# Three output blocks of the inner feed-forward layers in turns, each turn a scheduled step, and a new table of places

## The reference, cut to what matters

```python
def reference(x, ...):                         # x: (4, 1024, 256), fp32
    x = x + 0.5 * ffn(layernorm(x))
    x = x + attn(layernorm(x))
    x = x + 0.5 * ffn(layernorm(x))            # the same weights again
    return x

def ffn(x):                                    # weights are -1, 0 or 1, with one scale for each output
    h = silu((x @ w1.T) * s1) * ((x @ w2.T) * s2)      # 256 -> 1024
    h = gelu((h @ h1.T) * t1)                          # 1024 -> 1024, the first inner layer
    h = gelu((h @ h2.T) * t2)                          # 1024 -> 1024, the second inner layer
    return (h @ w3.T) * s3                             # 1024 -> 256

def attn(x):                                   # 16 heads of 16; each row looks back at 24 fixed offsets
    q, k, v = split(x @ Wqkv + bqkv)
    p = softmax(q . k[row - offset] / 4 + pos_bias)    # offsets 0 .. 768, causal
    return (sum(p * v[row - offset]) * sigmoid(x @ Wgate + bgate)) @ Wout + bout
```

## Time and profile before

| what | value |
|---|---|
| time, median of 3 runs | 1644.64 us (1642.39 to 1644.68) |
| the profiled execution's own time | 1643.29 us |
| its span | 1641.1 us |
| PE busy | 1514.2 us, 92% of the span |
| DVE, ACT, POOL busy | 66%, 41%, 34% |
| weights through the ring | 256 fills of 512 KB |

### The profile page before, as it was taken

How to read it: one execution, slowest core, us unless ns; L and a number is a source line. 1 busy time by engine, 2 the same in 40 slices (tenths; PEclk the granted TensorE clock), 3 DMA queues, 4 the chain that set the end, 5 groups by cost and what they waited for, 6 DMA issues and landing times.

```text
span 1641.1 us, 19144 instructions
## 1 busy us (share of the span) xinstructions
PE 1514.2 (92%) x6914; PEld 1215.0 (74%) x6914; DVE 1088.8 (66%) x1477; ACT 678.3 (41%) x1061; POOL 553.5 (34%) x402
## 2 busy tenths in 40 slices
PE   0399999999999999999999999889999999998998
PEld 0288787778777778787777777768788877776887
DVE  4423678886587867777977775869675978783322
ACT  4434344434343435444424343434343534342442
POOL 0111142516044425243426152351705254425020
PEclk9999999999999999999999999999999999999999
DMA  9633657676657575666855667547574766754332
GB/s 376 259 118 119 210 169 255 226 249 213 208 188 268 171 258 192 228 239 205 308 181 203 209 203 241 189 164 266 180 253 153 283 238 210 271 191 145 131 99 76
DMA packets 191008, 342.38 MB, mean 209 GB/s; under 512 B 15552, under 2 KB 138560, under 8 KB 190784
## 3 DMA queue, kind: packets, MB, share of 16 engines
q1 hardware_dynamic: 190912, 341.13, 60.9%
HBM read 310.66 MB, written 30.41 MB: 208 GB/s over the span
## 4 chain that ended last, share of the span: by engine, by line
PE 74%; DVE 9%; POOL 7%; DMA 4%; issue 3%; ACT 3%; SPq 0%; DVEq 0%; POOLq 0%; ACTq 0%
PE f_bank L1020 25%; PE f_bank L1021 24%; PE a_bank L1096 6%; PE f_bank L981 5%; PE f_bank L982 5%; PE f_bank L1049 3%; POOL acc L630 3%; PE f_bank L1050 3%; DMA slot<-in_ffn_w 2%; PE a_bank L1114 2%; DVE S L886 2%; DVE slot L880 2%; POOL acc L627 1%; POOL h_lo L644 1%; DVE slot L924 1%
## 5 line engine op out<-in xcount | busy, mean ns | idle before, releaser
L1020 PE MATMUL f_bank<-h_hi,wring 128*128 128x512 f32 x2048 | 824.6, 403 | 21.7 <-POOL h_lo L644 12.0
L1021 PE MATMUL f_bank<-h_lo,wring 128*128 128x512 f32 x2048 | 814.0, 397 | 0.0
L1020 PEld LDWEIGHTS f_bank<-h_hi,wring 128*128 128x128 f32 x2048 | 388.0, 189 | 120.2 <-POOL h_lo L644 16.1
L1021 PEld LDWEIGHTS f_bank<-h_lo,wring 128*128 128x128 f32 x2048 | 388.0, 189 | 93.7 <-issue 1.7
L714 ACT ACTIVATE h_hi<-f_bank,colv 128x512 fp32r<-128x512 f32 x256 | 176.0, 688 | 537.0 <-PE f_bank L1021 536.6
L840 DVE TENSOR_TENSOR h_lo<-f_bank,h_hi 128x512 fp32r<-128x512 f32 x256 | 175.4, 687 | 255.3 <-ACT f_bank L715 253.9
L644 POOL TENSOR_TENSOR h_lo<-f_gated,h_hi 128x512 fp32r<-128x512 f32 x128 | 166.3, 1311 | 501.0 <-ACT h_hi L708 500.8
L981 PE MATMUL f_bank<-fT_hi,w_in 128*128 128x512 f32 x512 | 212.1, 414 | 27.1 <-issue 10.9
L982 PE MATMUL f_bank<-fT_lo,w_in 128*128 128x512 f32 x512 | 206.1, 402 | 0.0
L924 DVE TENSOR_TENSOR slot<-slot,a_bank 128x1280 f32<-128x1280 f32 (+4 forms) x124 | 169.8, 1376 | 20.2 <-DMA slot<-keys_and_values 20.0
L880 DVE TENSOR_TENSOR slot<-slot,a_bank 128x1280 f32<-128x1280 f32 (+4 forms) x124 | 170.6, 1375 | 16.3 <-DMA slot<-keys_and_values 16.1
(11 more groups left out here) (92 smaller groups left out, 1191.4 us busy)
## 6 DMA issues: line engine op xcount, KB each, us to landing
wring<-weights_hi SPq DMA_DIRECT2D x256, 512.0 KB, 4.7
slot<-keys_and_values SPq DMA_DIRECT2D x128, 384.0 KB, 4.7
slot<-keys_and_values SPq DMA_DIRECT2D x64, 640.0 KB, 4.2
slot<-keys_and_values SPq DMA_DIRECT2D x312, 128.0 KB, 4.5
slot<-keys_and_values SPq DMA_DIRECT2D x64, 256.0 KB, 5.5
slot<-in_ffn_w SPq DMA_DIRECT2D x22, 512.0 KB, 6.8
weights_hi<-h_hi SPq DMA_DIRECT2D x16, 512.0 KB, 6.1
keys_and_values<-kv_out SPq DMA_DIRECT2D x32, 256.0 KB, 2.7
```

Source lines behind the costliest of these rows:

```text
L1020: pe.matmul(bank[:, :], hi, h_hi[src][:, k, :], start=(k == 0), stop=False)
L1021: last = pe.matmul(bank[:, :], hi, h_lo[src][:, k, :], start=False, stop=(not general and k == KH - 1))
```

## The change

`f_hidden` of the first three blocks of each inner layer is cut in two steps. A new PE step `f_begin` (r, layer, m) for m = 0, 1, 2 does k = 0..5 (12 matmuls); then the steps `f_hidden` m = 0, 1, 2 do k = 6, 7 (4 matmuls each). Before, one step held 28 matmuls (m = 0 and 1), then 4, then 16; now there are steps of 12, 12, 12, 4, 4, 4. Since attention steps are put in at boundaries of PE steps, they may now stand between these. The waits are those of before, and stand with the first part of a block; the number of matmuls is the same, and so is every transfer. The ring's fill times follow `f_begin`. `f_gelu`, `f_lo` of m = 0 and 1 and `f_stats` follow the later planned end of m = 0 and 1. `TIMES`, `FOLLOW` and `STARTS` have new numbers, of which these lines are a part.

```diff
-TIMES = [4.0, 9.6, 11.1, 13.4, 16.0, 24.8, 22, 3.8, 5.6, 53.0, 58.4, 3.1, 86.9, 3.5]
+TIMES = [3.8, 9.6, 11.1, 16.4, 18.6, 27.1, 23.3, 3.8, 6.4, 53.0, 60.2, 3.3, 89.2, 3.5]
-FOLLOW = dict(silu=-1.5, gate=0.1, cut=1.3, low=2.0, gelu=-0.4,
-              lo=1.0, residual=-1.5, residual2=0.4, fill=20.7, stats=0.1, turn=4)
+FOLLOW = dict(silu=-1.5, gate=-0.4, cut=1.3, low=1.3, gelu=-0.4,
+              lo=1.3, residual=-1.5, residual2=0.2, fill=20.7, stats=0.0, turn=4)
...
+    ABREAST = 3
...
                 for layer in range(2):
+                    for m in range(ABREAST):
+                        pe(2.8, "f_begin", r, layer, m)
                     for m in range(KH):
-                        done = pe([6.5, 0.95, 3.7][min(m, 2)], "f_hidden", r, layer, m)
+                        done = pe(0.95 if m < ABREAST else 3.7, "f_hidden", r, layer, m)
+                        if m < ABREAST:
+                            begin["f_hidden", r.j, layer, m] = begin["f_begin", r.j, layer, m]
...
-            def run_hidden(r, layer, m, ring, general):
+            def run_hidden(r, layer, m, early, ring, general):
...
-                if general or m > 1:
-                    part(m, 0, KH)
-                elif m == 0:
-                    part(0, 0, EARLY)
-                    part(1, 0, EARLY)
-                    part(0, EARLY, KH)
+                if general:
+                    if not early:
+                        part(m, 0, KH)
+                elif early:
+                    part(m, 0, EARLY)
                 else:
-                    part(1, EARLY, KH)
+                    part(m, EARLY if m < ABREAST else 0, KH)
```

More of the change, by code:

```diff
@@ L30 @@
          "z", "out"]
-TIMES = [4.0, 9.6, 11.1, 13.4, 16.0, 24.8, 22, 3.8, 5.6, 53.0, 58.4, 3.1, 86.9, 3.5]
-FOLLOW = dict(silu=-1.5, gate=0.1, cut=1.3, low=2.0, gelu=-0.4,
-              lo=1.0, residual=-1.5, residual2=0.4, fill=20.7, stats=0.1, turn=4)
-STARTS = [86, 164, 237, 328, 401, 468, 552, 632,
-          703, 783, 862, 941, 1021, 1102, 1173, 1251]
+TIMES = [3.8, 9.6, 11.1, 16.4, 18.6, 27.1, 23.3, 3.8, 6.4, 53.0, 60.2, 3.3, 89.2, 3.5]
+FOLLOW = dict(silu=-1.5, gate=-0.4, cut=1.3, low=1.3, gelu=-0.4,
+              lo=1.3, residual=-1.5, residual2=0.2, fill=20.7, stats=0.0, turn=4)
+STARTS = [86, 164, 237, 328, 401, 468, 554, 632,
+          703, 781, 862, 938, 1027, 1102, 1173, 1251]
 class Counts:
@@ L1122, in run @@
                     "f_in": lambda r, m: run_in(r, m, ring, general),
-                    "f_hidden": lambda r, layer, m: run_hidden(r, layer, m, ring, general),
+                    "f_begin": lambda r, layer, m: run_hidden(r, layer, m, True, ring, general),
+                    "f_hidden": lambda r, layer, m: run_hidden(r, layer, m, False, ring, general),
                     "f_out": lambda r: run_out(r, ring, general),
```

## The result

The changed kernel takes 1653.77 us in the median of 5 runs (1652.39 to 1657.51), the kernel before 1644.68 us (1642.39 to 1646.13): a ratio of 1.0056, 95% interval 1.0042 to 1.007. It is slower by 9.1 us (0.6%), where a gain of 3.7 was forecast.

What follows compares the result with a forecast made beforehand. PE, busy 92%, was taken as the bound, with 81 us between its matmuls to act on. Gains of 28.4 us less costs of 24.7 net 3.7, giving 1640.9 us from the median; forecast range 1634 to 1648, overall 1625 to 1654.

Steps and rivals of the forecast that it cites:

- pass 14, `f_low` 7: POOL does `f_low` 7 straight behind `f_low` 6, so PE's wait and half-rate loss there go: gain 9.0 us.
- second residual: End of pass 3: the second `f_residual` now precedes a score, shortening waits into pass 4: gain 3 us, bounds 1 to 4.5.
- pass 9 to 10, and 321, 819: Layer 1's block 4 waits less behind a10's scores, gain 4 us; similar waits at 321 and 819, gain 3 together.
- pairs at once: PE waits out evictions when `a_turn` meets kv0 or `a_z_turn` its `a_out`; 9 pairs become 16: cost 5.2 us.
- `a_tanh`: Passes 8 and 13: ACT does `a_tanh` ahead of `f_scale`, so `f_turn` waits: cost 7 us, 3.5 each.
- `a_exp`: Passes 5 and 10: `a_exp` and table loads come between `f_gelu` 1 and 2, delaying `f_scale` and `f_turn`: cost 4.5 us.
- a11's `a_turn`: Pass 10: reached 24 matmuls into the layer instead of 48, so PE waits for `a_hat`: cost 4 us, bounds 0 to 7.
- ring: Slot 0 is freed later while block 4 is due as before, giving waits of 1.1 and 0.4: cost 1 us.
- Rival C: Ring fills queue behind SP's other waits, 26 layers x 0.3 us at block 4: no difference, 1649 us; chance 0.08.
- Rival B: Reordered ACT and POOL steps decide, new gaps bring half-rate windows: slower, about 1651 us; chance 0.22.
- Rival A: New stalls are swallowed, since PE's waits let DVE and POOL catch up: about 1630 us; chance 0.25.
- Rival D: The third block does nothing without a late `f_low`, leaving only the places; already in the sum, no chance of its own.

Runs made afterwards that it cites:

- e4: The changed kernel with `f_scale` ahead of `a_tanh` in passes 8 and 13, on ACT's order alone: 1649.78 us, 1.0034.
- e5: The changed kernel with `f_stats`, `f_rstd` and `f_scale` planned 2.8 us earlier (stats=-2.8): 1650.7 us, 1.0031.
- e15: The changed kernel with three blocks in turn in layer 0 and only two in layer 1: 1645.44 us, 1.0001.
- e3: The changed kernel with two blocks in turn instead of three, as steps of their own, new places kept: 1645.01 us, 0.9997.
- e6: The changed kernel with `f_stats`, `f_rstd` and `f_scale` planned 4.1 us earlier (stats=-4.1): 1665.29 us, 1.0113.
- e8: The changed kernel with stats=-4.1 and the ring's transfers for blocks 4 and 12 planned 3.2 us earlier in SP's order: 1665.53 us, 1.0126.
- e12: The changed kernel with the third block doing only k = 0 to 3 in its turn, so block 0 ends 0.93 us earlier: 1640.4 us, 0.9968.
- e13: The changed kernel with a third block of 4 k in its turn and `f_turn` one block later (turn=5): 1634.84 us, 0.9936.
- e18: The changed kernel with a third block of 2 k in its turn and `f_turn` one block later (turn=5): 1633.14 us, 0.9928.
- e9: The changed kernel with `f_turn` one block later (turn=5) and the bank waits that belong to it: 1641.76 us, 0.9981.

## Why the prediction was wrong

Each term, with what the changed kernel's trace gives. A gap is counted here, as in the expectations, from start to start of PE's instructions less the undisturbed pace, which is 0.1 to 0.2 us more than the idle time in brackets. Gaps and the clock behind them are counted together; a stretch of 3.41 us at half rate is 1.7 us.

| step of the prediction | forecast | found |
|---|---|---|
| pass 14, `f_low` 7 | gain 9.0 | 9.0: no wait near 1480, no half-rate stretch |
| pass 9, cover | gain 1.4 | 1.4: one wait for POOL is left, in pass 5 |
| second residual | gain 3 | 4.6: in pass 4 4.55 us became 1.60, and its stretch is gone; pass 3 waits 0.8 longer |
| pass 11 | gain 4.5 | 3.4: 1.7, 2.5 and a stretch became 1.6 and 1.0 |
| pass 9 to 10, and 321, 819 | gain 7 | 13: 4.5, 2.0 and 3.7 became 0.7, 0 and 2.2, and three stretches (1.7, 1.7 and 2.2 us) went |
| `a_z_turn` and `a_turn` | gain 3.5 | 0.4 |
| pairs at once | cost 5.2 | 4.3 (waits for aT and zT) |
| `a_tanh` | cost 7 | 7.2 in the trace; undone, 3.6 (e4) |
| `a_exp` | cost 4.5 | 8.0: 2.80 twice with two stretches, less 1.0 of before |
| a11's `a_turn` | cost 4 | 7: 4.7, then 1.0 twice and smaller ones at half rate |
| a2, a4 | cost 3 | 3.3 |
| ring | cost 1 | 9.4: 6.0 and two stretches |
| not in the sum | 0 | `f_turn` of passes 4 and 12: 5.1; a6's `a_turn`: 3.8; pass 5: 1.4 |

The gains come to 32 us against 28.4, the costs to some 50 against 24.7. The difference, 18, is more than the 12.4 measured in the trace; the 5 us between are short waits that became shorter, and are not listed.

Nearly every sign that was to show the prediction right came: pass 14 at full clock, the wait for POOL in pass 5, waits for `f_hat` in passes 5, 8, 10 and 13, 4.5 us for `a_hat` in pass 10. One that was to show it wrong came too, the waits for `wring`. Most of what was priced was priced well; most of the loss is in what was put at nothing or, for the ring, at 1 us.

**The step that failed** is the last sentence of the ring's paragraph: that the burst of three blocks takes 0.5 us of the reserve of `f_scale` and of block 4 of layer 1, "which costs nothing there". It counted what the third block adds for ACT and DVE at the end of block 0 and not that the end itself is 2.8 us later, for everything that is due at `f_turn` and block 4. That sentence stood beside the right one for the ring, where the 2.8 us were subtracted. The runs show in its place: five waits ahead of `f_turn` that go when the statistics go back by 2.8 us (e5, for 4.1 us of time, since others came in their place), and 9.0 us of time that return when layer 1 has two blocks in turn (e15), 9.7 when both layers have (e3). The other failing step is the ring's size: its reserve of 1.7 us was read from layers in which the transfer was 3.3 us; the three that waited took 4.4 to 6.2 us and went out 1.0 to 2.9 us late behind slot loads, in passes in which a sub-tile's scores or weighing run beside them. Rival C had this mechanism, in 26 layers for 0.3 us each; it came in three layers, with 2 us each. The ring's waits alone do not make the loss, since e15 has them in full.

**Rival B** is nearest to what came: 1651 forecast, 1653.8 measured, the number in part by luck. It named the half-rate stretches behind new gaps as the thing that decides, and a11's `a_turn`. Of its five new gaps four have a stretch behind them (the one in pass 8 has none), but so have gaps that it did not count, at the ring's waits and in pass 6; and the gain of the gaps at 321, 819 and 1030, which it had as absent, came with 13 us. Its reason, reordered ACT and POOL steps, covers half of it. Of POOL's new order only the 1.4 us in pass 5 are seen.

**Rival A**, the swallowed waits, is true of single edits and not of the sum. e4 returned 3.6 of 7.2 us, e5 4.1 of 14.5 (each good to some 3), e6 to e8 less than nothing. The change was forecast by adding up waits, and for edits within one engine's order such a sum overstated by about two or more here. The edits that gave back about what their waits promised, or more (e12: 14.5 us where 8 to 12 were expected; e13 and e18), left the window longer or moved what was due at its end; e9, of the second kind, gave half.

**Rival D**, that the third block does nothing, has it the wrong way round: with the new places it is the part that costs, and without it the time is that of before (e3).

Small operations of DVE that a POOL instruction holds up, which the earlier trace rows showed for a11, are in the new kernel too, at the head of the same chains. DVE in pass 7, where POOL's 1.30 us instruction from 821.12 ends at 822.42:

```profile
821.11 0.16 DVE L752 TENSOR_TENSOR f_mo<-f_st 128x4 f32<-128x4 f32 x1
821.30 1.15 DVE L754 TENSOR_SCALAR f_mean<-f_mo 128x4 f32<-128x4 f32 x1
822.36 0.15 DVE L755 TENSOR_TENSOR f_mo<-f_mo 128x4 f32<-128x4 f32 x1
```

The Trainium skill (SBUF — State Buffer, section "SBUF: two separate sides") has the port pair that the two engines share as a lock held for a whole instruction; the trace agrees for this operation, which ends when POOL's does, after 1.15 us instead of the 0.16 of its neighbours.

## What to carry to other kernels

When a piece of work is put ahead of another, list all that hangs on the end of the other and all that is due at a fixed place behind it, on every engine and queue; the window between the two has shrunk for each of them, and an order that helps one takes it from the next. The remedy is to move what is due, or to lengthen the cover only as far as the window bears; here that turned a loss of 0.6% into a gain of 0.7 to 0.8%. Waits read from a trace did not tell what an edit to one engine's order returns: here it was between less than nothing and half of them.

## What the runs showed of the hardware

The clock at half rate (PEclk 0.50) followed gaps shorter than the 2.7 us that Rival B had counted with, but not surely. In the changed kernel single gaps of 1.9 to 2.0 us of idle time (at 524.56, 669.58, 794.77 and 1508.06) have a stretch of 3.41 us behind them; others of 1.9 us (356.73, 497.33) and one of 2.1 (828.48) have none. The same gap can go either way: in e4 the 1.9 us at 670.52 have no stretch behind them, and the 2.1 us at 825.54 have one. In e12 the gaps ahead of `f_turn` in passes 4 and 5 are 1.3 and 1.7 us instead of 1.9 and 2.6, and have lost the stretches that the changed kernel has there. Shortening a wait from 2.6 to 1.7 us was worth 2.6 there.

In the profiled executions half rate is a large part of what the waits cost: up to the last matmul it stands for 41 us in the changed kernel and for 24 in e12. These 17 us are worth up to 8.5, as much as the idle time that e12 has less (56.2 us instead of 64.6), and the two executions are 15.3 us apart.

Repeated runs of one kernel spread over 10 us, with the mean granted clock: beside e5 the kernel before took 1649.8 us at 0.983 and 1640.2 us at 0.990. A good part of the scatter of one program seems to be how many of its gaps have the half rate behind them; that was not tested by itself.
